# Another order of the values in device memory for criss-cross attention

## The reference: what is computed

```python
q = einsum('bchw,oc->bohw', x, Wq) + bq      # 64 channels
k = einsum('bchw,oc->bohw', x, Wk) + bk      # 64 channels
v = einsum('bchw,oc->bohw', x, Wv) + bv      # 512 channels
eH = einsum('bchw,bcpw->bhwp', q, k)         # along the column; the pixel itself is masked
eW = einsum('bchw,bchp->bhwp', q, k)         # along the row
att = softmax(concatenate([eH, eW], axis=3), axis=3)
attH, attW = att[..., :H], att[..., H:]
outH = einsum('bcpw,bhwp->bchw', v, attH)
outW = einsum('bchp,bhwp->bchw', v, attW)
return gamma * (outH + outW) + x
```

## Time and profile before

| | |
|---|---|
| median of 3 runs | 4418.41 us |
| lowest and highest run | 4412.54 and 4428.46 us |
| the profiled execution | 4430.1 us |
| its span | 4428.3 us |
| granted clock of TensorE over the span | 0.86 of full speed |
| TensorE (PE) busy | 3545.5 us, 80% |
| VectorE (DVE) busy | 2586.0 us, 58% |
| ScalarE (ACT) busy | 1875.7 us, 42% |
| GpSimd (POOL) busy | 1246.6 us, 28% |
| moved between memories | 1179.35 MB in 824051 packets, mean 266 GB/s |

### The profile page before, as it was taken

One profiled execution on the slowest core, in us unless ns is written; L12 is line 12 of the kernel. 1 busy time (PEld: TensorE's weight loads), 2 busy tenths in 40 slices (PEclk: granted clock), 3 DMA queues, 4 the chain that ended last, 5 costly groups with the idle time before them and its releaser, 6 DMA issues.

```text
span 4428.3 us, 97049 instructions
## 1 busy us (share of the span) xinstructions
PE 3545.5 (80%) x33624; PEld 2431.6 (55%) x33624; DVE 2586.0 (58%) x3802; ACT 1875.7 (42%) x3852; POOL 1246.6 (28%) x1075
## 2 busy tenths in 40 slices
PE   3987978778887887878977798878988778884865
PEld 1544755456564564645655466554755456563755
DVE  6546764477554774538745576455765477554643
ACT  1545634165241752427532474325634165242621
POOL 0000341404413044220433214240241404413333
PEclk9998799888898798997999879889799888996665
DMA  7958688986989779996899968899689986999399
GB/s 273 297 187 276 209 275 263 326 279 197 312 259 315 255 200 307 289 315 224 240 303 310 302 206 257 273 325 292 208 272 268 330 280 194 316 261 286 96 288 287
DMA packets 824051, 1179.35 MB, mean 266 GB/s; under 512 B 56560, under 2 KB 574192, under 8 KB 823536
## 3 DMA queue, kind: packets, MB, share of 16 engines
q1 hardware_dynamic: 509136, 831.94, 61.5%
q10 hardware_dynamic: 314400, 340.86, 24.0%
HBM read 832.83 MB, written 339.74 MB: 265 GB/s over the span
## 4 chain that ended last, share of the span: by engine, by line
issue 33%; DMA 26%; PE 21%; POOL 10%; DVE 4%; SPq 3%; ACT 2%; ACTq 1%; POOLq 0%; DVEq 0%
DMA xr<-x 23%; POOL acc L496 4%; PE banks L1033 4%; PE banks L1034 4%; PE banks L1035 4%; POOL prob_col L486 4%; PE banks L1107 3%; PE banks L1109 2%; PE banks L1108 2%; DMA v_in<-v_pixel_major 2%; POOL qk_pair L468 2%; SPq L377 1%; DVE floor L770 1%; PE banks L1085 1%; DMA x_first<-x 1%
## 5 line engine op out<-in xcount | busy, mean ns | idle before, releaser
L1033 PE MATMUL banks<-wv_hi,x_hi 128*128 128x512 f16 x2304 | 936.2, 406 | 247.9 <-DVE x_lo L804 247.8
L812 DVE SCALAR_TENSOR_TENSOR v_out<-banks,proj,v_out 128x512 f16<-128x512 f32 x576 | 431.2, 749 | 1076.7 <-ACT v_out L591 1075.8
L496 POOL TENSOR_TENSOR acc<-acc,xr 128x768 f32<-128x768 f32 x384 | 716.3, 1866 | 878.0 <-DMA xr<-x 700.5
L1034 PE MATMUL banks<-wv_lo,x_hi 128*128 128x512 f16 x2304 | 930.1, 404 | 0.0
L1035 PE MATMUL banks<-wv_hi,x_lo 128*128 128x512 f16 x2304 | 924.5, 401 | 0.0
L591 ACT ACTIVATE v_out<-banks,proj 128x512 f16<-128x512 f32 x576 | 390.8, 684 | 970.3 <-PE banks L1035 968.9
L468 POOL TENSOR_TENSOR qk_pair<-qk_f,qk_pair 128x256 f16<-128x256 f32 x288 | 202.6, 703 | 2034.4 <-ACT qk_pair L607 2027.2
L1107 PE MATMUL banks<-prob_row,v_in 96*128 96x96 f16 x3072 | 475.0, 217 | 309.9 <-DMA v_in<-v_pixel_major 259.9
L893 DVE SCALAR_TENSOR_TENSOR acc<-banks,att,acc 128x384 f32<-128x384 f32 x768 | 443.1, 609 | 266.6 <-PE banks L1109 265.9
L1033 PEld LDWEIGHTS banks<-wv_hi,x_hi 128*128 128x128 f16 x2304 | 237.6, 103 | 519.7 <-issue 314.7
L1107 PEld LDWEIGHTS banks<-prob_row,v_in 96*128 96x128 f16 x3072 | 318.8, 104 | 367.0 <-issue 229.6
(11 more groups left out here) (104 smaller groups left out, 7055.4 us busy)
## 6 DMA issues: line engine op xcount, KB each, us to landing
v_in<-v_pixel_major SPq DMA_DIRECT2D x768, 384.0 KB, 7.1
x_raw<-x ACTq DMA_DIRECT2D x290, 512.0 KB, 6.9
x_next<-x SPq DMA_DIRECT2D x384, 384.0 KB, 3.7
v_pixel_major<-v_out ACTq DMA_DIRECT2D x576, 256.0 KB, 4.0
xr<-x SPq DMA_DIRECT2D x384, 384.0 KB, 9.5
out<-acc SPq DMA_DIRECT2D x384, 384.0 KB, 8.6
qk_halves<-qk_pair ACTq DMA_DIRECT2D x288, 128.0 KB, 4.1
x_first<-x SPq DMA_DIRECT2D x24, 768.0 KB, 9.0
```

The source lines that it names most:

```text
L496: nc.gpsimd.tensor_tensor(acc[tt][:, px], acc[tt][:, px], xr[n % XR][:, :], ALU.add).then_inc(res_added, 1)
L812: nc.vector.scalar_tensor_tensor(out=v_out[tile % V_OUT][:, :, 1, :], in0=bank[tile % 2][:, :].rearrange("p (t c) -> p t c", t=CT), scalar ...
L1033: nc.tensor.matmul(dst, s_hi, m_hi, start=(t == 0), stop=False)
L1034: nc.tensor.matmul(dst, s_hi, m_lo, start=False, stop=False)
```

## The change

The array of values gets another order: image, pair of channel tiles (one pass's half), image column, image row, and then the 512 float16 numbers (1 KB) of that pixel and pair. Three things follow in the code.

- The load of a row group has four image rows one after the other in memory, which is one piece of 4 KB on each of 96 partitions in place of four of 1 KB. The load of a column group still has four pieces of 1 KB on each partition, now 96 KB apart.
- The store of a v tile writes two pieces of 1 KB for each pixel, in place of one of 2 KB. The 128 pixels of a tile always lie in two image rows of 96, so the store becomes two transfers, of 96 and 32, 64 and 64, or 32 and 96 pixels.
- Both transfers count on the same semaphore, whose waits go up by 32 for each use of a buffer.

```diff
--- before.py
+++ after.py
@@ -86,11 +86,15 @@
     x_scan = x.rearrange("b (p k) h w -> b p (k h w)", p=P)
     out_acc = out.rearrange("b (t c) h w -> b t c (h w)", c=P)
 
-    vT = nc.dram_tensor("v_pixel_major", [B, HW, CT * 2 * P], F16, kind="Internal").ap()
-    vT_load = {
-        ROW: vT.rearrange("b (h w) (y a) -> b y w h a", w=W, y=TP),
-        COL: vT.rearrange("b (h w) (y a) -> b y h w a", w=W, y=TP),
-    }
+    vT = nc.dram_tensor("v_column_major", [B, TP, W, H, TT * 2 * P], F16, kind="Internal").ap()
+    vT_load = {ROW: vT, COL: vT.rearrange("b y w h a -> b y h w a")}
+    vT_store = vT.rearrange("b y w h a -> b h w y a")
+
+    def fragments(px):
+
+        return [(row, max(px, row * W), min(px + P, (row + 1) * W)) for row in range(px // W, (px + P - 1) // W + 1)]
+
+    assert all(len(fragments(px)) == 2 for px in range(0, HW, P))
     qk = nc.dram_tensor("qk_halves", [B, 2, P, HW], F16, kind="Internal").ap()
 
     qk_store = qk.rearrange("b a p n -> b p a n")
@@ -321,7 +325,7 @@
         @block.sync
         def _(sp):
             for k in range(V_OUT):
-                sp.sem_inc(v_stored[k], 16)
+                sp.sem_inc(v_stored[k], 32)
             for s in range(2):
                 sp.sem_inc(qk_stored[s], 16)
             for tt in range(TT):
@@ -389,7 +393,7 @@
                     for c in range(NXT):
                         load_next((b + 2) % B, b + 1, c)
                 for t in range(V_OUT):
-                    wait_alone(sp, v_stored[t], (b + 1) * (ROUNDS["v"] * 16) + 16)
+                    wait_alone(sp, v_stored[t], (b + 1) * (ROUNDS["v"] * 32) + 32)
                 wait_alone(sp, o_mm, b * GROUPS + ONE0)
                 for n in range(VU):
                     load_v(b, n)
@@ -564,10 +568,12 @@
                 tile = n * PT + j
                 k = tile % V_OUT
                 act.wait_ge(v_ready, m * (NB * PT) + tile + 1 + V_READY0)
-                act.dma_start(
-                    vT[m, n * BLK + j * P:n * BLK + (j + 1) * P, :],
-                    v_out[k][:, :, :, :].rearrange("p t a c -> p (t a c)"),
-                ).then_inc(v_stored[k], 16)
+                px = n * BLK + j * P
+                for row, first, end in fragments(px):
+                    act.dma_start(
+                        vT_store[m, row, first - row * W:end - row * W, :, :],
+                        v_out[k][first - px:end - px, :, :, :].rearrange("p (y t) a c -> p y (t a c)", y=TP),
+                    ).then_inc(v_stored[k], 16)
 
             def store_qk(m, n):
                 act.wait_ge(qk_ready, m * NB + n + 1 + QK_READY0)
@@ -587,7 +593,7 @@
                 tile = n * PT + j
                 k = tile % V_OUT
                 act.wait_ge(v_mm, m * (NB * PT) + tile + 1)
-                act.wait_ge(v_stored[k], m * (ROUNDS["v"] * 16) + (tile // V_OUT) * 16 + 16)
+                act.wait_ge(v_stored[k], m * (ROUNDS["v"] * 32) + (tile // V_OUT) * 32 + 32)
                 nc.scalar.activation(
                     v_out[k][:, :, 0, :], bank[tile % 2][:, :].rearrange("p (t c) -> p t c", t=CT), ACT.Copy,
                     scale=proj[:, EVAC_V:EVAC_V + 1],
```

## The result

| | before | after |
|---|---|---|
| median (4 runs each) | 4416.35 us | 4510.52 us |
| lowest and highest | 4412.54 to 4428.46 | 4486.11 to 4531.99 |
| profiled execution, span | 4428.3 us | 4499.8 us |

The ratio is 1.0207, with a 95% interval of 1.0147 to 1.0266. The change made the kernel 2.1% slower; the forecast was 2.2% faster.

What follows compares the result with a forecast made beforehand. The prediction took full DMA queues in the row halves as the bound. Row loads -148, stores +45 and ACT's issues +7 made -96 us, from 4418.4 to 4322 us; range 4262 to 4430, leaving out a tenth each side.

Steps and rivals of the forecast that it cites:

- What bounds the kernel: Row halves: DMA queues are full, so a row half is as long as its transfers take and shorter transfers shorten it.
- What a packet costs: DMA loads: 27.6 ns for each packet plus 35.4 ns for each KB, giving 169 ns for a 4 KB piece.
- The line: DMA load cost drawn through 63 ns for 1 KB and 240 ns for 6 KB pieces; 169 ns for 4 KB.
- dear end: Row loads: 4 KB pieces at 233 ns, by bytes from q and k's loads, saving only 44 us in all.
- the mixture of rows 8: Last image's row half: 1 KB and 3 KB pieces priced by the line at 81 us, against a stretch of 82.
- The store of a tile: Stores where queues are full: more packets cost 0.15 us a tile, 45 us in all (0 to 75).
- ACT's issues: Scores: the second issue of each store delays exponentials the matrix engine waits for; 1 us an image, 7 us in all.
- the term's upper end: ACT's issues at most: 8 tiles x 0.5 us x 7 images = 28 us.
- Its sign: What would show ACT's issues: a longer score stage.
- The sum: Whole kernel: -148 + 45 + 7 = -96 us, from 4418.4 to 4322 us.
- the slower one: Rival, stores on ACT's queue: two parts use too few partitions, a tile costs one store more; 4515 us, chance 0.10.
- The first rival: Loads: packets cost little, 1 KB loads are slow for their 96 partitions, 4 KB near 233 ns; 4399 us, chance 0.18.

Runs made afterwards that it cites:

- e4: The changed kernel with each row load bringing 512 KB to 128 partitions in 4 KB pieces, in place of 384 KB to 96: 4431.7 us, ratio 1.0025.
- e13: The kernel before with the second tile's store issued behind the next x and row loads on 128 partitions in 1 KB pieces: 4337.2 us, ratio 0.9830.
- e3: The changed kernel with row loads as four 1 KB pieces on each of 96 partitions, in place of one of 4 KB: 4516.7 us, ratio 1.0214.
- e2: The changed kernel with each tile's store issued once, over 128 partitions, in 1 KB pieces: 4414.4 us, ratio 0.9989.
- e10: The kernel before with each tile's store still one issue, but in pieces of 1 KB in place of 2 KB: 4422.9 us, ratio 1.0026.
- e1: The kernel before with only the store of a tile issued as two transfers, order of values and loads unchanged: 4478.4 us, ratio 1.0140.
- e5: The kernel before with a second, nearly empty transfer (16 partitions x 32 bytes) behind each tile's store on ACT's queue: 4476.8 us, ratio 1.0118.
- e15: The kernel before with each tile's store split by channels into two transfers of 128 partitions, one 1 KB piece each: 4478.9 us, ratio 1.0149.

## Why the prediction was wrong

- **What bounds the kernel:** right. The row halves waited for full queues; e4 and e13 shortened them by faster transfers (the 14 row halves from 1191 us to 1109 and 1124).
- **What a packet costs: the step that failed.** The line was laid through v's 1 KB pieces, which go to 96 partitions, and `x_first`'s 6 KB pieces, which go to 128. The difference was booked to the size of the piece. It was the spread: a 4 KB piece on 96 partitions took 267 ns in after and not 169, on 128 partitions 166 in e4, and e3 equals after. The "dear end", q and k on 64 partitions, was the row with the right lesson, and 233 ns was nearer, yet it was given a fifth of the chance. That the line met the mixture of rows 8 was no test, because the mixture had the same 1 KB pieces on 96 partitions, and 3 KB pieces close to the line's middle. Predicted 148 us; measured none that can be told from nothing, the most favourable pair of runs giving some 16 us (e2 beside e10): after's last image has 144.7 against 144.1 us, and the 10 us or so that the 14 halves with items gave back are there without the new loads too (e1, e5).
- **The store of a tile:** 45 us for its pieces was too much (e10: 11).
- **ACT's issues: the other step that failed.** 7 us, measured 57 to 60. The sum asked only whether the matrix engine waits for exponentials, and said that elsewhere ACT waits for matmuls. It did so before (20.8 us in 130 to 250 by the waits), but that wait stands before `v_out`, and the issues stand before the next block's `x_hi`. With the second issue ACT's wait for matmuls fell to 7.6 us and the matrix engine's for `x_lo` rose from 1.3 to 12.9. Even the term's upper end, 28 us, was short: it counted 8 tiles an image of 72. Its sign, a longer score stage, did not show (670 against 667 us); the loss lay in the other stretches with items.
- **The sum:** the terms that failed are 148 against about 0, 45 against 11 and 7 against 57 to 60. The measured ones make some 70 of the 94 us lost; the rest is open (e3 beside e15).
- **The rivals:** the slower one named 4515 us, near the measured 4510, with 0.10, and for the wrong reason: its two parts were to take as long as two stores. e5 has most of the loss with 16 partitions x 32 bytes. So naming a time near the measured one was luck. By the rule of the Trainium skill quoted beside it (DMA: Bandwidth & Descriptors, "Rules for kernel authors"), two transfers to disjoint halves of the partitions share the same 16 engines and serialize. e1 and e5 (1.0140 and 1.0118) agree with it as far as they go: splitting the bytes cost little on the engines, the issuing engine paid. The first rival had the loads nearly right (233 ns, 267 measured), but not the stores (4399 us in all). The third, 4272, leaves out the 7 us for ACT; with them it would be 4279.

A rule of the Trainium skill may stand behind the spread (DMA: Bandwidth & Descriptors, section on the descriptor swizzle): in a transfer to 128 partitions each DMA engine writes to one port, and the page works this out for 128 partitions only. The measured 403 against 310 GB/s do not contradict it. That ports are the cause no run here shows; 64 partitions at a fixed size of piece was not tried.

## What to carry to other kernels

Before two rows are compared for the size of their pieces, see that they agree in all else, in the number of partitions above all: here 128 partitions in place of 96 were worth 34 to 80 us, so that even loading a third more, unread, was faster, while 4 KB in place of 1 KB was worth nothing clear on 96 partitions and 36 to 49 us on 128. Count a transfer's issue as an instruction of its engine, and look what stands behind it in that engine's order. Here moving one issue by one step was worth 18 us without the split and 50 to 60 with it, against 11 for the size of the pieces. A layout that turns one store into two is paid at each store, not where the loads are.

## What was not expected of the hardware

- 512 KB to 128 partitions in 4 KB pieces are faster than 384 KB to 96: row halves of 64.0 and 65.6 us against 74.2 and 70.5 in the last image, 403 against 310 GB/s.
- On 96 partitions the size of the piece hardly counts (4517 us with 1 KB, 4511 with 4 KB; 252 and 267 ns for 4 KB); on 128 it does (4468 and 4432 us; 200 and 166 ns).
- A transfer of 512 bytes in all, issued 576 times on ACT, costs 57 us of 4420 (by the ratio 52), 0.1 us each on average, although ACT is busy 42% of the time.
